# Self-attention of a decoder: softmax sums in ScalarE's exponentials instead of products with ones

## The reference

```python
def _L1_attn_ref(x, W_in, b_in, W_out, b_out):
    qkv = x @ W_in + b_in
    q, k, v = jnp.split(qkv, 3, axis=-1)
    q, k, v = (heads(q), heads(k), heads(v))
    scores = jnp.einsum('bhsd,bhtd->bhst', q, k)
    scores = jnp.where(mask, -jnp.inf, scores)      # causal
    scores = scores / jnp.sqrt(Dh)
    probs = jax.nn.softmax(scores, axis=-1)
    out = jnp.einsum('bhst,bhtd->bhsd', probs, v)
    return out.transpose(0, 2, 1, 3).reshape(B, S, D) @ W_out + b_out

x = x + _L0_attn_ref(_layernorm(x), ...)     # a linear mixer
x = x + _L0_xattn_ref(_layernorm(x), ctx, mask)
x = x + _L0_ffn_ref(_layernorm(x), ...)      # ternary weights, 8-bit rounded activations
x = x + _L1_attn_ref(_layernorm(x), ...)
x = x + _L1_xattn_ref(_layernorm(x), ctx, ...)
x = x + _L1_ffn_ref(_layernorm(x), ...)      # 32 masked experts, one a token
```

## Time and profile before

| | us |
|---|---|
| median of 3 runs | 1186.63 |
| lowest, highest | 1184.1, 1187.51 |
| profiled execution, its own time | 1187.17 |
| span of its trace | 1184.3 |
| TensorE busy | 1041.7 (88%) |
| VectorE busy | 877.1 (74%) |
| ScalarE busy | 653.8 (55%) |
| GpSimd busy | 326.3 (28%) |
| mean granted TensorE clock | 0.947 |

### The profile page before, as it was taken

One profiled execution on the slowest core, in us unless ns is written; L12 is line 12 of the kernel. 1 busy time (PEld: TensorE's weight loads), 2 busy tenths in 40 slices (PEclk: granted clock), 3 DMA queues, 4 the chain that ended last, 5 costly groups with the idle time before them and its releaser, 6 DMA issues.

```text
span 1184.3 us, 21508 instructions
## 1 busy us (share of the span) xinstructions
PE 1041.7 (88%) x6293; PEld 716.7 (61%) x6301; DVE 877.1 (74%) x2458; ACT 653.8 (55%) x2010; POOL 326.3 (28%) x528
## 2 busy tenths in 40 slices
PE   7788886898999957899999999999999999988395
PEld 5654445676666634565766756657666666666385
DVE  5777774778877767877877878878878788764285
ACT  2777783655555524556556565565565645741262
POOL 3342222111111321312323223223232232101465
PEclk7979997999999978899999999999999999999598
DMA  9710001111111004000000000000000000000731
GB/s 286 251 35 2 1 1 54 55 55 54 53 53 53 19 1 133 26 1 14 1 14 1 1 14 1 5 10 1 16 1 0 14 1 0 15 1 24 263 99 45
DMA packets 38875, 49.58 MB, mean 42 GB/s; under 512 B 5110, under 2 KB 29564, under 8 KB 38528
## 3 DMA queue, kind: packets, MB, share of 16 engines
q1 hardware_dynamic: 36160, 44.16, 12.4%
q0 software_dynamic: 2304, 4.24, 1.0%
q10 hardware_dynamic: 320, 0.15, 0.1%
HBM read 32.70 MB, written 14.78 MB: 40 GB/s over the span
## 4 chain that ended last, share of the span: by engine, by line
PE 47%; ACT 4%; issue 4%; POOL 4%; DVE 3%; DMA 0%; DVEq 0%; ACTq 0%; POOLq 0%
PE PS L1842 41%; POOL out_dram L1417 3%; PE PS L2229 2%; PE PS L2209 2%; ACT arena L1682 1%; POOL tokens_dram L1393 1%; PE PS L2086 1%; DVE arena L823 1%; ACT arena L1691 1%; DVE arena L859 0%; DVE arena L847 0%; ACT early L1618 0%; PE PS L2231 0%; PE PS L2274 0%; PE PS L1852 0%
## 5 line engine op out<-in xcount | busy, mean ns | idle before, releaser
L1842 PE MATMUL PS<-early,arena 128*32 128x128 f32 (+6 forms) x920 | 122.2, 361 | 46.0 <-DVE early L713 23.7
L1842 PE MATMUL PS<-EW,arena 128*128 128x256 f32 (+7 forms) x512 | 121.2, 360 | 16.8 <-DVE small L847 7.3
L1842 PE MATMUL PS<-wq,EW 128*128 128x512 f32 x256 | 125.7, 614 | 6.8 <-DVE arena L823 6.6
L1331 POOL TENSOR_SCALAR small<-small 128x4 f32<-128x4 f32 x64 | 18.6, 291 | 385.2 <-ACT mask L1675 215.5
L1842 PEld LDWEIGHTS PS<-early,arena 128*32 128x32 f32 (+4 forms) x928 | 62.4, 121 | 99.8 <-issue 38.0
L847 DVE CUSTOM_DVE_ANT_0 arena<-PS,kmask 128x128 f32<-128x128 f32 (+3 forms) x256 | 91.4, 389 | 41.4 <-PE PS L1842 35.9
L1691 ACT ACTIVATE arena<-arena,small 128x128 f32<-128x128 f32 (+3 forms) x256 | 119.5, 473 | 0.5 <-DVE small L852 0.3
L1842 PE MATMUL PS<-wo,early 128*128 128x256 f32 x512 | 115.0, 384 | 3.6 <-DVE sinT L900 2.8
L1842 PEld LDWEIGHTS PS<-EW,arena 128*128 128x128 f32 x512 | 83.5, 193 | 43.7 <-issue 23.0
L1842 PEld LDWEIGHTS PS<-wo,early 128*128 128x128 f32 x512 | 98.6, 193 | 17.7 <-DVE sinT L900 3.2
L1682 ACT ACTIVATE arena<-PS 128x512 f32<-128x512 f32 x64 | 38.2, 597 | 114.5 <-PE PS L2209 114.1
(11 more groups left out here) (343 smaller groups left out, 2435.7 us busy)
## 6 DMA issues: line engine op xcount, KB each, us to landing
EW<-in_masksT_dram SPq DMA_DIRECT2D x32, 256.0 KB, 3.5
tokens_dram<-EW SPq DMA_DIRECT2D x1, 4160.0 KB, 16.1
arena<-tokens_dram SPq DMA_DIRECT2D x16, 260.0 KB, 2.8
results_dram<-EW SPq DMA_DIRECT2D x32, 128.0 KB, 3.2
EW<-results_dram SPq DMA_DIRECT2D x4, 1024.0 KB, 10.5
X<-in_x_dram SPq DMA_DIRECT2D x8, 256.0 KB, 5.1
wq<-in_wq_dram SPq DMA_DIRECT2D x1, 2048.0 KB, 11.1
wo<-in_wo_dram SPq DMA_DIRECT2D x1, 2048.0 KB, 18.5
```

The source lines that it names most:

```text
L1842: return pe.matmul(dst, lhs, rhs, start=first, stop=last)
```

## The change

- Each exponential of the self-attention also gives the sum of its row (`accum_out`), into d_sum, 32 columns of a small tile. The eight products with ones of each unit, the tile d_ones and its four memsets go.
- A new step on VectorE, `self_reciprocals(b, m)`, takes 16 reciprocals a row and copies each 16 times into dR. TensorE turns dR, two transposes behind the outputs of the odd unit, into the columns of bank 6 where the sums stood.
- `self_normalise` copies these from PSUM (instead of the reciprocal) and multiplies.
- `self_reciprocals` of group 0 stands behind the normalisation at i = 2, of group 1 at i = 0 of the next batch, ahead of the normalisation. Even units of ScalarE wait for the reciprocals that read the cells they overwrite.
- In the head, four of the bias steps go to ScalarE (`bias_round`), two stay on VectorE one n later (`bias_rest`); `cross_normalise` moves ahead of the constants at n = 4 and of `prepare` at n = 7; three of the six roundings of weights move ahead of the cross exponentials.
- `keep_going(n)` issues n products of ones with ones whose result nobody reads: 8 and 3 at the start, 4 ahead of the cross turn for n = 4, 5 and 6, 10 for n = 7, 4 before and 4 behind the first level turn.

```diff
+        dR = cut(3584, (J * P // DH, DH), F32, early); dRT = cut(3840, (S,), F32, early)
+        d_sum = small[:, 52:84].rearrange("p (m j r e) -> p m j r e", m=2, j=J, r=4); d_inv = small[:, 84:100]
...
-                dve.reciprocal(dR, PS[:, 6, S:2 * S]).then_inc(d_r, 1)
-                dve.wait_ge(d_r, 2 * b + m + 1)
+                dve.tensor_copy(dRT, PS[:, 6, S:2 * S]).then_inc(d_rt, 1)
+                dve.wait_ge(d_rt, 2 * b + m + 1)
                 after(dve, d_y, b)
-                dve.tensor_tensor(dOT[:, m, :], PS[:, 6, 0:S], dR, ALU.mult).then_inc(d_o, 1)
+                dve.tensor_tensor(dOT[:, m, :], PS[:, 6, 0:S], dRT, ALU.mult).then_inc(d_o, 1)
+
+            def self_reciprocals(b, m):
+
+                dve.wait_ge(d_e, 4 * (4 * b + 2 * m + 2))
+                after(dve, d_r, 4 * b + 2 * m)
+                dve.reciprocal(d_inv, d_sum[:, m].rearrange("p j r e -> p (j r e)")).then_inc(d_r, 1)
+                dve.wait_ge(d_r, 4 * b + 2 * m + 1)
+                after(dve, d_pv, 4 * b + 2 * m)
+                dve.tensor_copy(dR, bc(d_inv.unsqueeze(2), [P, J * P // DH, DH])).then_inc(d_r, 1)
...
                     if i == 0:
                         if former:
+                            self_reciprocals(b - 1, 1)
                             self_normalise(b - 1, 0)
...
                     if i == 2:
                         if former:
                             self_normalise(b - 1, 1)
+                        self_reciprocals(b, 0)
...
             self_normalise(B - 1, 0)
+            self_reciprocals(B - 1, 1)
             self_turned(4 * B - 1, 3)
...
+                    if i % 2 == 0:
+                        after(act, d_r, 4 * b + i - 3)
+                    m, e = i // 2, i % 2
                     for r in range(4):
-                        act.activation(dP[:, i % 2, r, 0:P], PS[:, r, 0:P], ACT.Exp, bias=d_neg[:, i % 2, 0, r:r + 1])
+                        act.activation(dP[:, i % 2, r, 0:P], PS[:, r, 0:P], ACT.Exp, bias=d_neg[:, i % 2, 0, r:r + 1],
+                                       accum_out=d_sum[:, m, 0, r, e:e + 1])
                         act.activation(dP[:, i % 2, r, P:3 * P], PS[:, r, P:3 * P], ACT.Exp,
-                                       bias=d_neg[:, i % 2, 1, r:r + 1]).then_inc(d_e, 1)
+                                       bias=d_neg[:, i % 2, 1, r:r + 1],
+                                       accum_out=d_sum[:, m, 1, r, e:e + 1]).then_inc(d_e, 1)
...
-                for summed in range(2):
-                    for k in range(2):
-                        for r in range(4):
-                            weights = d_ones[:, e, :] if summed else dV[:, par, k, 8 * m + 2 * r + e, :]
-                            last = product(PS[2 * DH * r:2 * DH * (r + 1), 6, summed * S + k * P:(summed + 1) * S], weights,
-                                           dPT[:, i % 2, r, 2 * P * k:2 * P + P * k], e + k + summed == 0, e + k + summed == 3)
+                for k in range(2):
+                    for r in range(4):
+                        last = product(PS[2 * DH * r:2 * DH * (r + 1), 6, k * P:S], dV[:, par, k, 8 * m + 2 * r + e, :],
+                                       dPT[:, i % 2, r, 2 * P * k:2 * P + P * k], e + k == 0, e + k == 2)
+                if e == 1:
+                    pe.wait_ge(d_r, 4 * b + 2 * m + 2)
+                    for j in range(J):
+                        last = pe.transpose(PS[:, 6, S + j * P:S + (j + 1) * P],
+                                            dR[:, j * P // DH:(j + 1) * P // DH, :].rearrange("p h d -> p (h d)"), ident[:, :])
                 last.then_inc(d_pv, 1)
...
+            def keep_going(n, at=6):
+
+                for _ in range(n):
+                    product(PS[:, at, 0:P], ones[:, :], ones[:, :])
+
...
+                if n >= 4:
+                    keep_going(10 if n == B - 1 else 4, 4)
                 if n >= 1:
                     cross_turn(n - 1)
...
-                for i in {4: (0, 1), 5: (2, 3), 6: (4,), 7: (5,)}.get(n, ()):
+                for i in {4: (0,), 5: (2,), 6: (4,)}.get(n, ()):
                     rounding(i)
+                if n in (4, 5, 6):
+                    bias_round(n - 4)
```

More of the change, by code:

```diff
@@ L1294, in _ @@
             pool.memset(dV.rearrange("p a j h d -> p (a j h d)"), 0.0).then_inc(d_zero, 1)
-            for e in range(2):
-                for k in range(2):
-                    pool.memset(d_ones[:, e, k * DH:(k + 1) * DH], 1.0 if e == k else 0.0).then_inc(d_zero, 1)
             scale_rows(1)
@@ L1508, in rounding, with bias_round @@
                 act.activation(w, w, ACT.Identity, bias=magic[:, 0:1], scale=rgam[:, i // 2:i // 2 + 1]).then_inc(s_clip, 1)
+            def bias_round(k):
+                act.wait_ge(s_c, mark["unit"] if k == 0 else mark[f"rest{k - 1}"])
+                if k == 0:
+                    act.wait_ge(s_l2, 16 * 5)
+                    act.activation(biasF, biasF, ACT.Copy, scale=g_unit).then_inc(s_prep, 1)
+                    act.wait_ge(s_prep, PIECES + 1)
+                if k < 2:
+                    act.activation(biasV, biasF, ACT.Copy).then_inc(s_prep, 1 + k)
+                else:
+                    act.activation(biasB, biasF, ACT.Copy, scale=g_any).then_inc(s_prep, 1)
             def cross_exps(b):
@@ L1530, in head @@
                     magnitude(i)
+                for i in {5: (1,), 6: (3,), 7: (5,)}.get(n, ()):
+                    rounding(i)
                 if n == B:
@@ L1868, in level_turn @@
                 last.then_inc(s_xtp, 1)
+            def keep_going(n, at=6):
+                for _ in range(n):
+                    product(PS[:, at, 0:P], ones[:, :], ones[:, :])
             pe.wait_ge(s_pc, 2)
-            for _ in range(10):
-                product(PS[:, 6, 0:P], ones[:, :], ones[:, :])
+            keep_going(10)
             pe.wait_ge(s_l0, 16 * 7)
@@ L1948, in head_end @@
             def head_end():
+                keep_going(4, 4)
                 level_turn(0)
+                keep_going(4, 4)
                 pe.wait_ge(s_tern, 2 * (PIECES // 3))
[L1952 removed]
+                pe.wait_ge(s_prep, PIECES + 5)
                 pe.wait_ge(s_x, added(MIX, B - 1))
```

47 lines of the change are left out of this document (22 added, 25 removed).

## The result

In one set of runs on one chip the changed kernel took a median of 1188.73 us (20 runs) and the kernel before 1185.41 us (20 runs): ratio 1.0032, 95% interval 1.0019 to 1.0045. The forecast was 1183.4 us, a little faster. The profiled execution took 1187.06 us (before: 1187.17) with a span of 1185.1 us.

The account below looks back on a forecast made before the run. TensorE bounds the self-attention only in part; VectorE and a scores-to-exponentials ring through single-set PSUM banks also limit it. Loop +4.5, behind it -4.7, head -3.0: -3.2 on 1187.17, 1184.0, median 1183.4 us; range 1176 to 1195.

Parts of the forecast that it names:

- The ring: Self-attention: scores, maximum reduction, exponentials, next scores through four PSUM banks without a second set; 6.21 becomes 6.91 us, binding every unit.
- the reads: Self-attention, ScalarE: accumulator read instructions behind the exponentials, priced from the next stage's squares at 0.70 us a unit.
- The rival that let the exponential pay its full length: Self-attention: accumulating costs 1.0 us or slightly more a unit instead of 0.70; +9, 1192.5 us; chance 0.14.
- the free accumulation: Self-attention: accumulating costs nothing and the ring stays at 6.21 us; 1164 us in all; chance 0.05.
- The loop's sum: Self-attention loop: six middle batches +3.2, first batch +2.3, last batch -1.0; together +4.5 us.
- Behind the loop: After the self-attention loop: shorter normalisations and fewer ones products, half a chance of full-clock output product; -4.7, ends -3.9 and -5.5.
- The rival of a copy held by GpSimd: Self-attention unit 0: the dR copy is delayed, VectorE binds at 7.4 us; +3, 1186 us; chance 0.08.
- The clock in the loop: Self-attention: emptier TensorE falls to half clock, scores take some 0.7 us longer; +7, 1190.5 us; chance 0.09.
- The head: Program start to feed-forward: filling products keep mixers at full clock and bias steps leave VectorE; -3 us, ends -6 and +2.
- the bad case: Head at half clock at 56: four fillings take 1.7 us before a ready cross turn, n = 7 pays 0.6; about 1 later.
- The start: Beginning of the head: fillings (8 and 3) can keep the first mixer fast; between 0 and 1.8 us, taken at 1.
- The rival of fillings in front of ready work: Head stays at half clock and filling products stand in the way: +1 instead of -3, 1187.4 us; chance 0.14.

Follow-up runs that it names:

- the shortened ring: Changed kernel with the maxima taken and announced for two PSUM banks at a time, so exponentials start after the first half: 1175.82 us, ratio 0.9916 to the kernel before.

## Why the prediction was wrong

**The ring.** Predicted 6.91 us, taken as 7.0, 7.0, 6.91 and 6.91; measured 7.02, 6.94, 6.99 and 6.95, 27.90 a batch for 27.8. The value of 0.70 us a unit for the reads, taken from the squares of the earlier trace rows, was 0.73 (3.33 - 2.60). The rival that let the exponential pay its full length (1.0 us) is out, as is the free accumulation. This step was right, and so was its consequence that 24 and 28 us of removed work buy nothing in the loop.

**The loop's sum.** +4.5 predicted, +5.4 in the pair and +5.8 in the mean. The terms were mis-sized by little each: six middle batches by 0.62 instead of 0.54 are 3.7 for 3.2, the first batch gave 2.5 for 2.3 (28.54 for 25.99), the last -0.8 for -1.0 (21.37 for 22.15).

**Behind the loop.** -4.7 predicted, -4.9 in the pair, -4.5 in the mean. The waits came out at 7.66 and 1.07, each about 1.4 shorter for 1.33. From the last reduction to the end of the product by w_out, which leaves the unchanged 750 us out, it is 25.8 to 20.4 us in the pair, -5.4 for the forecast end of -5.5, and -4.1 in the mean. Whether that product meets full clock, which was left half open, is indeed open: it took 1.97 us in 6 of the 14 executions with the change and in 1 of the 6 without, else 3.3 to 3.75. The step was right; that the pair had 1.97 is luck.

**The copy into dR.** The rival of a copy held by GpSimd was seen: 0.78 us in unit 0, against 0.29 at 298.95 in unit 2, with GpSimd multiplying beside the first:

```profile
282.31 5.02 POOL L1316 TENSOR_TENSOR EW<-EW,ew 128x512 bf16<-128x512 f32 x4
...
298.95 0.29 DVE L722 COPY early<-small 128x256 f32<-128x256 f32 x1
```

It did not bind, since the ring was longer; unit 0 was 7.02 and not 7.4. The Trainium skill, SBUF — State Buffer, section "Who interferes with whom", says that a copy can take the port pair that VectorE shares with GpSimd and that the second comer waits for the whole instruction. The trace agrees in kind. But GpSimd at work is not enough: with the shortened ring the copy took 0.30 inside GpSimd's multiplications (272.27, they last from 271.06 to 276.20), and there it is the layer norm's tensor_scalar, 2.41 us for two, that makes unit 0 the longest.

**The clock in the loop.** It stayed at 1.00 in the 190 us though TensorE's share fell to 82%. That rival is out.

**The head: the step that failed.** Predicted -3.0 with ends of -6 and +2; measured at the first reduction +0.3 in the pair and -0.3 in the mean, and at the turn in the feed-forward, which leaves most of that unchanged stretch out, +0.35 and -1.0. The failed step is the claim that at n = 5 "a mixer at full clock ends 1.8 us earlier and the four cost 0.85, so the cross turn behind comes 0.95 earlier; the same at n = 6, and about 1.5 more in the scores and transposes up to the feed-forward: 3.4 us". From n = 3 on the mean gain is 1.5 us, and 1.3 of it is there without any filling. Term by term, means of before against changed:

- n = 5: 0.3 us lost instead of 0.95 won. The forecast read one execution, in which the mixer of 56.60 was at half clock, as the state of the kernel. In three of six executions it was at full clock already; and between these two states the turn moves by 0.6 us and not 1.8, since it waits next for VectorE's normalisation. Against a mixer at half clock the fillings do win 0.85 at this turn (3.57 to 2.72), near the 0.95; against the kernel before as it is on average (8.34 us from turn to turn), little is left. In the pair the mixer did take 2.40 us (58.40), but its four products held the turn back from 60.60 to 62.31, 1.71 us and not 0.85.
- n = 4: not in the sum. The moved steps win 1.3 us there and the fillings cost 0.98.
- n = 6: 1.5 won for 0.95, the same with and without fillings.
- Behind it: 0.7 lost up to n = 7, where ScalarE's moved steps had been priced (0.6) for the bad case alone, and 0.6 won from there to the feed-forward, for 1.5 won. The kernels with the steps alone lose the 0.7 too (7.20 for 6.37); which of the steps costs it is not shown.
- The start: taken at 1 us won. The first mixer did take 1.99 instead of 3.75, and the second started 3.0 us earlier in the pair (16.21 for 19.21). Nothing of it is left at n = 3: 43.7 us in the mean for 43.3. In the pair the turn of n = 3 came 2.0 us later (45.91 for 43.88), with the mixer of 35.76 at 3.76 us where that of 34.81 had 2.00.

Nor does the sum add up as written: the terms spelt out are 1.0 and 3.4, and how 3.0 comes of 4.4 and the bad case is not worked out. The rival of fillings in front of ready work was given 0.14 and only for a head at half clock. It happens at full clock too (0.98 us at n = 4), though at their single size the fillings earn it back one n later. What is left to explain between -1.0 at the turn and -0.3 at the first reduction lies in the feed-forward, 93.2 to 93.9 us, inside the spread of one program.

**The outcome.** By the means, 2.7 us of error ahead of the first reduction, 1.3 in the loop and 0.2 behind it turn -3.2 into +1.0. The other 2 to 3 us of the first set of runs belong to no step that I can name. The range of 1176 to 1195 held the time, but the side was wrong.

## What to carry to other kernels

Before counting what an edit takes off an engine, write down the ring that ties the engines together through a buffer with no second set, and ask on which side of it the edit puts its cost: 0.09 us per instruction inside the ring outweighed 52 us outside it. An edit that empties engines is worth something only together with one that shortens the ring; try the pair, since each alone can measure as nothing. Filling products for the clock cost nothing only where TensorE's next input is late by more than they last, and the row that shows it is the producer's end against the consumer's start; what they bring has to be read further on, at the products that they keep at full clock. Read a stretch whose clock changes from execution to execution in several of them before pricing it, and at a landmark close behind the edit.

## What the runs showed of the hardware

- A filling set in front of ready work costs its own time (0.98 us for four products at full clock, at n = 4), and can bring as much back at a later product that it keeps at full clock (the mixer of n = 5, 1.99 to 2.40 us for 3.61 to 3.78, 0.85 us at the turn behind it). A doubled set added 4.1 us and no clock. The mean granted clock over the span is 0.958 to 0.960 in the kernels with the steps and all fillings and 0.953 to 0.956 in those with the steps and none, and from n = 3 on the head takes 58.0 us with them and 58.2 without. The Trainium skill, TensorE: Matmul & The Clock Gate, section "Why this matters for your kernels", advises to keep TensorE busy so that it runs at its full clock. The granted clock agrees here; the time of the whole does not follow it.
- An exponential from PSUM pays the same for its accumulator read as a square does: 0.09 us between starts, though the read's own row says 0.19 to 0.24.
- Sets of runs of one and the same text differ by up to 0.4% in their ratio to the same kernel, more than their 95% intervals say, and the executions differ in where the half-clock stretches of the head and of the first batch fall.
